# Last group of a routed FFN: sums made in the expert slots and scattered to their rows, in place of gathers

## What is computed

```python
mod = (silu(c) @ wmod).reshape(8, 6, 1, -1)          # sa, ca, ga, sb, cb, gb
h = layernorm(x) * (1 + ca) + sa
x = x + ga * attn_ref(h)     # x1: SSM and GRU scanned over 512 steps, then mixed by two gates
h = layernorm(x) * (1 + cb) + sb
p = softmax(h @ gate_w.T); e = argmax(p)
x = x + gb * p[e] * (relu(h @ w1[e] + b1[e]) @ w2[e] + b2[e])
```

## Time and profile before

| | us |
|---|---|
| runs shown: median of 3 (lowest to highest) | 693.38 (693.11 to 694.08) |
| the profiled execution's own time | 694.49 |
| its span in the trace | 692.6 |
| TensorE busy | 671.2 (97%) |
| DVE / ACT / POOL busy | 522.9 / 422.3 / 120.0 |
| granted TensorE clock, mean | 0.992 |

### The profile page before, as it was taken

How to read it: one execution, slowest core, us unless ns; L and a number is a source line. 1 busy time by engine, 2 the same in 40 slices (tenths; PEclk the granted TensorE clock), 3 DMA queues, 4 the chain that set the end, 5 groups by cost and what they waited for, 6 DMA issues and landing times.

```text
span 692.6 us, 35329 instructions
## 1 busy us (share of the span) xinstructions
PE 671.2 (97%) x13692; PEld 630.6 (91%) x13692; DVE 522.9 (76%) x3189; ACT 422.3 (61%) x2677; POOL 120.0 (17%) x211
## 2 busy tenths in 40 slices
PE   7999999999999999999999999999999999999991
PEld 4899999989999999999999999999999999998891
DVE  4777777777787777888888778878887888876463
ACT  4555555556666666567666775676667656766540
POOL 3011111111011111112112211111212212221222
PEclk9999999999999999999999999999999999999996
DMA  8836000513522100044322000552210006433262
GB/s 300 304 116 237 8 6 8 216 41 124 194 94 87 53 15 15 14 164 174 132 77 82 19 18 19 201 178 95 94 61 22 22 19 243 151 114 132 74 224 57
DMA packets 46152, 72.79 MB, mean 105 GB/s; under 512 B 6236, under 2 KB 28834, under 8 KB 45858
## 3 DMA queue, kind: packets, MB, share of 16 engines
q1 hardware_dynamic: 41922, 65.11, 26.8%
q0 software_dynamic: 2048, 4.20, 2.1%
q10 hardware_dynamic: 2016, 1.25, 0.6%
HBM read 14.44 MB, written 21.17 MB: 51 GB/s over the span
## 4 chain that ended last, share of the span: by engine, by line
PE 95%; issue 1%; DVE 1%; DMA 1%; ACT 1%; POOL 0%; POOLq 0%
PE rs_bank L1183 34%; PE nz_bank L1183 23%; PE hid_bank_b L1183 12%; PE work L1183 11%; PE y_bank L1183 9%; PE hid_bank_a L1183 7%; DMA yg<-rows,pos 0%; POOL yg L694 0%; DMA rows<-y_sb 0%; ACT v_fac L793 0%; DVE mw L1096 0%; POOLq L498 0%; DVE fin_g L1168 0%; ACT hid_b L775 0%; DVE y_sb L1162 0%
## 5 line engine op out<-in xcount | busy, mean ns | idle before, releaser
L1183 PE MATMUL nz_bank<-h_ring,wg 128*64 128x16 f32 x4088 | 207.1, 211 | 0.0
L787 ACT ACTIVATE r_fac<-rs_bank 128x8 f32<-128x8 f32 x512 | 91.4, 178 | 169.3 <-PE rs_bank L1183 161.9
L1183 PEld LDWEIGHTS nz_bank<-h_ring,wg 128*64 128x64 f32 x4088 | 160.5, 136 | 1.3
L1183 PE MATMUL rs_bank<-mw,wg 128*64 128x8 f32 x2044 | 147.7, 213 | 1.0
L1183 PE MATMUL rs_bank<-s_ring,ws_sb 128*64 128x64 f32 x1024 | 141.8, 220 | 0.0
L1183 PE MATMUL rs_bank<-u,wg 128*64 128x8 f32 x2044 | 140.4, 206 | 0.1
L1183 PEld LDWEIGHTS rs_bank<-s_ring,ws_sb 128*64 128x64 f32 x1024 | 127.2, 136 | 9.4
L1092 DVE TENSOR_TENSOR_SCAN nz_bank<-r_fac,nz_bank 128x16 f32<-128x16 f32 x512 | 99.4, 194 | 46.6 <-ACT r_fac L787 29.6
L1096 DVE SCALAR_TENSOR_TENSOR mw<-v_fac,h_ring 128x8 f32<-128x8 f32 x512 | 85.7, 167 | 58.5
L1183 PEld LDWEIGHTS rs_bank<-mw,wg 128*64 128x64 f32 x2044 | 101.4, 134 | 19.1 <-DVE mw L1096 3.9
L793 ACT ACTIVATE v_fac<-nz_bank 128x8 f32<-128x8 f32 x512 | 90.7, 177 | 43.3
(11 more groups left out here) (162 smaller groups left out, 1074.8 us busy)
## 6 DMA issues: line engine op xcount, KB each, us to landing
wx<-w_all SPq DMA_DIRECT2D x59, 578.0 KB, 3.6
rows<-zeros SPq DMA_DIRECT2D x3, 4096.0 KB, 14.6
rows<-y_sb SPq DMA_DIRECT2D x67, 64.0 KB, 1.6
w_all<-in_w SPq DMA_DIRECT2D x2, 2048.0 KB, 16.0
xs_sb<-rows SPq DMA_DIRECT2D x55, 64.0 KB, 2.9
x_sb<-in_x SPq DMA_DIRECT2D x1, 1920.0 KB, 10.0
out<-o_sb SPq DMA_DIRECT2D x19, 64.0 KB, 2.3
out<-o_sb ACTq DMA_DIRECT2D x13, 64.0 KB, 1.9
```

What stands on the lines that cost most here:

```text
L787: nc.scalar.activation(r_fac[:, k, :, 1], r_cols(q, t), ACT.Tanh, scale=0.5).then_inc(rn_ready, 1)
L1183: last = nc.tensor.matmul(out[c:c + COLS], weights[:, c:c + COLS], moving, start=start, stop=stop, skip_group_check=skip_group_check)
```

## The change

The last group's five gathers go. Instead, what the final sum needs is brought to the slots.

- A side row of 257 floats goes with each token of tiles 27 to 31: x1, prob · gb, and the token's row number in the output. x1 is written straight into side (x1_of), ACT forms prob · gb there (side_gate), and POOL scatters the tile's side rows to side_rows in DRAM at the same pos as h2 (scatter_side).
- At step 160 SP fills all 8192 side rows with a row whose numbers mark it as no token. SP loads the side rows of slots 55 to 62 at step 538, ahead of the store of slot 54, and those of 63 to 66 with the extra slots' other loads.
- For each slot of the last group DVE adds b2 into y_last and, one step on, forms fin_last = y_last · (prob · gb) and o_last = fin_last + x1. Row numbers become scatter indices in two operations for slots 55 to 62 and two for 63 to 66 (tokens); rows of no token go to rows of their own behind the output.
- POOL scatters o_last of each slot to out_rows in DRAM (scatter_out), two steps after the slot's y. When all twelve have landed, SP copies the five tiles' part of out_rows to out, one DMA of 320 KB from DRAM to DRAM.
- y of slots 55 to 66 is no longer stored. The gathers of the fourth group stand 4 steps apart instead of 6. Of the last group the second half of A leaves by ACT, not DVE.

The diff, cut to its core:

```diff
@@ schedule
-            if k < NG - 1 and what[0] in "AC" and what[2]:
+            if what[2] and (what[0] == "A" or what[0] == "C" and k < NG - 1):
                 on_act.add(what)
@@ final_steps
-    for k in range(NG):
+    for k in range(NG - 1):
...
-                u = max(u, gather[FIRST[k] + i - 1] + (6 if k < NG - 1 else 3), NT * T + 13)
+                u = max(u, gather[FIRST[k] + i - 1] + 4, NT * T + 13)
...
+def side_at(j):
+    return (j + 2) * T + (10 if j < NT - 1 else 3)
+SIDE_LOADS = side_at(NT - 1) + 7
@@ SP
+            def load_side(n):
+                if n == FIXED0:
+                    eng.wait_ge(side_scattered, 16 * SIZE[-1])
+                at = fixed_expert(n) * GMAX
+                eng.dma_start(side_last[:, n - FIXED0:n - FIXED0 + 1, :],
+                              side_blocks()[:, at:at + 1, :]).then_inc(side_loaded[n - FIXED0], 16)
...
+                if t == 0 and c == 10:
+                    ge(eng, h_ready, u)
+                    eng.wait_ge(side_set, 4)
+                    eng.dma_start(side_blocks(), side_fill[:, :].unsqueeze(1).to_broadcast([P, BLOCKS, SIDE])
+                                  ).then_inc(side_filled, 16)
...
-                if u - 1 in Y_AT:
+                if Y_AT.get(u - 1, NSLOT) < FIXED0:
                     store_y(Y_AT[u - 1])
...
+                if u == SIDE_LOADS:
+                    for n in range(FIXED0, EXTRA0):
+                        load_side(n)
                 for n in load_at.get(u, []):
                     load_expert(n)
...
             steps(step)
+            eng.wait_ge(out_scattered, 16 * NLAST)
+            eng.dma_start(out[:, LAST * P:], out_rows.ap()[0:P * NT, :].rearrange("(p j) d -> p (j d)", j=NT)[:, LAST * P:]
+                          ).then_inc(last_stored, 16)
@@ POOL
+            def scatter_out(n):
+                m = n - FIXED0
+                eng.wait_ge(token_step, 2 if m < E else 4)
+                eng.wait_ge(out_ready, m + 1)
+                nc.gpsimd.indirect_dma_start(out_rows.ap(), index(token, m), o_last[:, m, :],
+                                             None).then_inc(out_scattered, 16)
...
+                    if j >= LAST and u == side_at(j) + 2:
+                        ge(eng, h_ready, min(u, NT * T))
+                        scatter_side(j)
-                    if u == GATHER_AT[j]:
+                    if j < LAST and u == GATHER_AT[j]:
                         ge(eng, h_ready, min(u, NT * T))
                         gather(j)
+                if Y_AT.get(u - 2, 0) >= FIXED0:
+                    scatter_out(Y_AT[u - 2])
@@ ACT
+                for j in range(LAST, NT):
+                    if g == side_at(j):
+                        ge(eng, prob_done, j + 1)
+                        nc.scalar.activation(side[:, j - LAST, P:2 * P], mod_gb, ACT.Copy,
+                                             scale=prob[:, j:j + 1]).then_inc(side_gate, 1)
@@ DVE
+            def tokens(first, end):
+                for m in range(first, end):
+                    eng.wait_ge(side_loaded[m], 16)
...
+                if Y_AT.get(g - 1, 0) >= FIXED0:
+                    n = Y_AT[g - 1]
+                    m = n - FIXED0
+                    eng.wait_ge(side_loaded[m], 16)
+                    ge(eng, y_ready, n + 1)
+                    nc.vector.tensor_tensor(fin_last[:, m, :], y_last[:, m, :], side_last[:, m, P:2 * P],
+                                            ALU.mult).then_inc(out_step, 1)
+                    if m in (0, E):
+                        tokens(m, E if m == 0 else NLAST)
+                    ge(eng, out_step, m + 1)
+                    nc.vector.tensor_tensor(o_last[:, m, :], fin_last[:, m, :], side_last[:, m, 0:P],
+                                            ALU.add).then_inc(out_ready, 1)
```

More of the change, by code:

```diff
@@ L73 @@
 NSLOT = SLOT0[NG]
+LAST = FIRST[-1]
+NLAST = SIZE[-1] + E - 1
+SIDE = 2 * P + 1
+NO_TOKEN = float(P * NT)
 DISPATCH_STEPS = 10
@@ L487, in adaln_kernel @@
         x_filled, xT_ready = sem("x_filled"), sem("xT_ready")
+        side_set, side_filled, side_gate, side_scattered = (
+            sem("side_set"), sem("side_filled"), sem("side_gate"), sem("side_scattered"))
+        side_loaded = [sem(f"side_loaded{b}") for b in range(NLAST)]
+        token_step = sem("token_step")
+        out_step, out_ready, out_scattered, last_stored = (
+            sem("out_step"), sem("out_ready"), sem("out_scattered"), sem("last_stored"))
         last_loaded = [sem(f"last_loaded{b}") for b in range(NSLOT - FIXED0)]
@@ L535, in blocks, with side_blocks, x1_of @@
             return rows[k % 3].ap().rearrange("(s p) d -> p s d", p=P)
+        def side_blocks():
+            return side_rows.ap().rearrange("(s p) d -> p s d", p=P)
+        def x1_of(j):
+            return x_sb[:, j * P:(j + 1) * P] if j < LAST else side[:, j - LAST, 0:P]
         def rows_bank(n):
@@ L614, in store_y @@
                 ge(eng, y_ready, n + 1)
[L615 to L616 removed]
+                eng.dma_start(blocks(k)[:, bass.ds(block_of.pop(n), 1), :], y_sb[:, b:b + 1, :]).then_inc(y_stored[b], 16)
             load_at = {}
@@ L1043, in place_rows @@
                     nc.vector.tensor_copy(pos[:, j:j + 1], pos_f[:, :]).then_inc(placed, 1)
+            def tokens(first, end):
+                for m in range(first, end):
+                    eng.wait_ge(side_loaded[m], 16)
+                own = side_last[:, first:end, 2 * P]
+                nc.vector.scalar_tensor_tensor(out=token_f[:, first:end], in0=own, scalar=NO_TOKEN,
+                                               in1=count[:, first:end], op0=ALU.is_ge, op1=ALU.mult).then_inc(token_step, 1)
+                eng.wait_ge(token_step, 1 if first == 0 else 3)
+                nc.vector.scalar_tensor_tensor(out=token[:, first:end], in0=token_f[:, first:end], scalar=float(P),
+                                               in1=own, op0=ALU.mult, op1=ALU.add).then_inc(token_step, 1)
             def lay_out(k, n):
@@ L1140, in step @@
                     tables(t)
+                if c == 2 and t == 0:
+                    eng.wait_ge(side_set, 2)
+                    nc.vector.tensor_scalar(side_fill[:, :], row_i[:, 0:1].to_broadcast([P, SIDE]), NO_TOKEN, None,
+                                            ALU.add).then_inc(side_set, 1)
+                if c == 2 and t == 1:
+                    nc.vector.tensor_copy(side[:, :, 2 * P], token_i[:, LAST:NT]).then_inc(side_set, 1)
                 for i in range(NT):
```

46 lines of the change are left out of this document (36 added, 10 removed).

## The result

| | before | after |
|---|---|---|
| median of 4 runs, us (lowest to highest) | 693.25 (692.95 to 694.08) | 700.53 (699.1 to 701.4) |
| ratio after to before, 95% interval | | 1.0101 (1.0082 to 1.012) |
| the profiled execution: own time / span | 694.49 / 692.6 | 699.10 / 697.3 |

What follows compares the result with a forecast made beforehand. TensorE bounds the kernel until 679, then a 13.6 us end without it. Tail to 689.4 plus 0.3 gives span 689.7 against 692.6; the 2.9 gain off median 693.38 gives 690.5 us, range 687.0 to 693.3.

Steps and rivals of the forecast that it cites:

- The scan: Recurrence before the tail: three gate products and two small DVE operations cost 0.3 us in all.
- Filling 8192 side rows: SP's fill at step 160: 29 us by bytes, 58 by pieces; slot 10's loads queue behind it; no cost unless over 45.
- The rival with a slow fill: A fill of 58 us at step 160 holds slot 10 some 13 us, total time 704 us or more; chance 0.03.
- From y54 to gather 20: Tail start: eight side loads on SP delay slot 54's y store, so tile 20's gather starts near 657.7, not 654.58.
- side loads hold the store on the DMA queue too: Tail start: tile 20's gather starts at 661.3, span 693.3, total 694.1 us, or 695.3 with the dear copy; chance 0.07.
- From gather 20 to the end: Tail: the span ends 31.7 us after tile 20's gather starts, with DVE's path deciding.
- The gather's data: Tail: tile 26's sum on DVE gets its gathered data 2.5 us after the gather's start, at 674.3.
- the wait that I had priced: DVE waits of the order of a us for tile 26's gather, delaying slot 64's relu; slot 66's y starts at 680.7.
- The slips of the earlier slots: TensorE loses 0.2 at slots 57, 59, 61, plus tiles 24 and 25's finals; 1.8 us, covered by tile 26's wait.
- The copy: Final 320 KB DRAM-to-DRAM copy: 3.2 us, bracket 1.9 to 4.4; with the program's close 4.65.
- gap of TensorE near 255: Named sign that the forecast is wrong: a TensorE gap near 255 us, where slot 10 would wait behind a slow fill.
- the first rival: Tail: DVE hardly waits; POOL's queue and TensorE's end decide: span 687.0 to 688.0, total 687.8 to 689.1; chance 0.22.

Runs made afterwards that it cites:

- e1: Kernel before plus only the fill of 8192 side rows, one 8.4 MB DMA at step 160, data unread: 702.5 us, ratio 1.0094.
- e5: Kernel before plus only the fill, split into 16 transfers of 512 rows, one every 8 steps from step 160: 693.84 us, ratio 1.0003.
- e10: Changed kernel, split fill, later side loads, eight gather buffers, later sums, gathers before scatters; final copy moves only tile 31's 64 KB: 691.69 us, ratio 0.9947.
- e2: Changed kernel with its fill split into 16 DMAs of 512 rows, 8 steps apart: 698.03 us, ratio 1.0037.
- e4: e2 with eight gather buffers instead of four, tile sums 20 steps behind gathers instead of 12, slot sums and scatters one step later: 693.91 us, ratio 0.9985.
- e11: Changed kernel with its single whole fill, but later side loads, eight gather buffers, later sums, gathers ahead of scatters: 699.26 us, ratio 1.0049.
- e15: Kernel before plus a quarter of the fill, 2.1 MB in rows of 1028 bytes, one transfer at step 160: ratio 1.0013.
- e16: Kernel before plus half the fill, 4.2 MB, as 8 transfers in a row at step 160: ratio 1.0044.
- e9: Kernel before plus half the fill, 4.2 MB in rows of 1028 bytes, one DMA at step 160: ratio 1.0107.
- e13: Kernel before plus one more fill at step 160, 4.19 MB of zeros in 2048-byte pieces: ratio 1.0078.

## Why the prediction was wrong, step by step

The predicted span was 689.7; it became 697.3. The 7.6 us between them divide into three:

- **The scan, 4.9 (0.3 priced, 5.2 measured). This is the step that failed:** "Filling 8192 side rows ... nothing, unless the fill takes over 45". I asked only who queues behind the fill on SP, found slot 10 with 48 us of room, and was right about that. I didn't ask who else uses the 16 DMA engines. The trace of before had the answer half in sight: queue q8, "instruction", among the DMA queues, and 4 MB fills that keep the engines full for 10 us, which turned out to be just short enough. The rival with a slow fill had the right part of the change but the wrong mechanism, a late slot 10, and chance 0.03. Nothing else in the scan was off by what the runs can tell: e1 has the loss with the fill alone, e5 none with the fill in pieces.
- **From y54 to gather 20, 0.95.** I had 6.05 from y54's completion; it was 7.0 (656.86 to 663.86). The mechanism, side loads ahead of the store, was right: before it was 2.93. The rival "side loads hold the store on the DMA queue too" put gather 20 at 661.3, 9.65 after y54, and is too dear: eight issues took 4.24, not 7.3.
- **From gather 20 to the end, 33.4 instead of 31.7.** POOL was right: 14.12 from gather 20 to gather 26 (14.1 said). Scatter and its landing were right, 2.23 (2.3). y66 to the last scatter 1.92 (1.75). Two terms were off. *The gather's data*, "2.5 after the gather's start", from a gather at the end of the program, where no load runs beside it: with the loads for slots 63 to 66 running it was 5.12 for tile 20 and 4.7 for tile 24. So DVE waited at tile 20 (2.55), where I had none, and not at tile 26. That gather 20 to y66 took 24.05 against my 23.0 is therefore luck: the wait that I had priced isn't there, and others stand in its place. The slips of the earlier slots, which I called covered by that wait, were not: y61 to y62 alone lost 1.2 us, across tile 24's sum. *The copy*, 4.65 with the close, was 5.24.

The copy's bracket by size, 1.9 to 4.4, rested on the idea that bytes set its price. e10 shows that from 64 to 320 KB they don't: the 1.9 us over the store's 3.35 are there with 64 KB as well. The Trainium skill, "DMA: Bandwidth & Descriptors", on the anatomy of one DMA, has 2.0 us plus bytes over 436e3 per us; the 256 KB less would be an estimated 0.6 us. That fit is for DMAs issued by GpSimd, and this copy is SP's. The rows show none of it, 5.2 in both, and the ratios are too coarse for it; the fixed part is larger for the copy than for the store that it replaced.

Right were the shape of the end (y66 to the last event 9.39, from 14.38; I had 8.7), POOL back to back, a wait of DVE for gathered data, and no gap of TensorE near 255. Without the fill (e2) the change would still have been slower by 0.37%, against a forecast of 0.4% faster; so the tail was misjudged as well, by some 5 us in the median of e2, more than its fastest run and the 2.7 us above show. Where a typical run of e2 loses the rest isn't shown; that e4 wins 0.52 points says that it is in DVE's waits for gathers, or in the order of DVE's sums and relus, which e4 changed with them. (A small slip in the first rival: its lower bound of 687.8 leaves out the scan's 0.3, which its upper bound has; no conclusion hangs on it.)

## What to carry to other kernels

Before adding a large DMA that "nobody waits for", look at how long it keeps all the engines full, and at who else lives on them: packets of instructions come that way. Cut it into pieces with gaps; 16 pieces of 0.5 MB cost nothing here where one transfer cost 6.5 us. Where an in-order engine feeds TensorE, don't put an operation that waits for a DMA ahead of the one that TensorE needs; putting these sums later was worth 0.52 points. In a full in-order queue, try what is ready early (the gathers) ahead of what becomes ready late (the scatters): here that gave 1.6 us in the median. Take an indirect gather's latency from a row that has the same traffic beside it.

## What was not expected of the hardware

- Beside a DMA stretch of 14 us and more at full engines TensorE stalled for 1.6 to 2.6 us with no semaphore in play, in all seven traces that have one (e11 has 2.55); beside 10 to 11 us it paused for 0.71 (e15) and 0.38 (the kernel before). The mechanism, a late packet of instructions, is inferred from the places of the packets, and why e16, full for 19 us, costs less than e9 stays open; each has four runs.
- The stall costs more than its length, since the granted clock may fall to 0.50 behind it, in the changed kernel for 10.2 us by the stretches (8 from 224 on, and 2.2 of the 4 before them for their mean of 0.72), though TensorE is busy all that time. In other traces it lasts 3.4 us (e9) to 20.5 (e11), counted in the same way. e13 shows how it differs from run to run of one program: of its ten runs four had a mean clock of 0.979 to 0.983 and took 701.3 to 702.4 us, five had 0.991 to 0.993 and took 694.6 to 697.3.
- A DRAM-to-DRAM copy closes the program 1.9 us later than a store of a tile from the chip's own memory does, whether it has 64 or 320 KB.
- An indirect gather's data took 2.5 us with the queue quiet and up to 5.1 beside loads.
